# Two-layer transformer on one core: in the first attention, the visible parts of two key tiles share one 128-column row of scores, and GpSimd takes the weights apart again; weights are split two steps ahead

## The reference, cut to what matters

```
x = x + attn0(layernorm(x))          # x is (4, 512, 256) float32
q = einsum('btd,ndh->btnh', x, q_kernel)            # 16 heads of 128
k, v = einsum('bsd,ckdh->cbskh', x, kv_kernel)      # 8 key/value heads
q, k = rope(rms_norm(q)), rope(rms_norm(k))
mask = (j <= i) & (i - j < 128)                     # causal, window of 128
logits = where(mask, (q * scale) @ k, lowest)
out = softmax(logits) @ v @ out_kernel
```

## Time and profile before

| | |
|---|---|
| median of 3 runs | 1585.34 us (1585.33 to 1596.49) |
| the profiled execution | 1583.67 us, of which its span 1581.4 us |
| PE busy | 92% of the span |
| DVE / ACT / POOL busy | 70% / 51% / 21% of the span |
| first attention | from the start to about 653 us |
| mean granted TensorE clock | 0.958 of full speed |

### The profile page before, as it was taken

The page is one execution under the profiler, slowest core; times in us unless marked ns, Lnnn a source line. Parts: engine busy times, 40 slices in busy tenths (PEclk is TensorE's granted clock), DMA queues, the critical chain, the costliest instruction groups (busy, mean ns, idle before and its releaser), DMA issues.

```text
span 1581.4 us, 24555 instructions
## 1 busy us (share of the span) xinstructions
PE 1452.6 (92%) x7806; PEld 1104.6 (70%) x7806; DVE 1112.8 (70%) x2356; ACT 810.5 (51%) x1983; POOL 334.4 (21%) x448
## 2 busy tenths in 40 slices
PE   3699999999999999799999999999849898989898
PEld 2589989988998899667777777777624344444376
DVE  5699899989998999377555455455437676767554
ACT  2466676666766767444332332332215464646566
POOL 3364454444444544000000000000012020201000
PEclk9899999999999999899999999999957899999999
DMA  4210000000000000233000000000052232222001
GB/s 130 67 41 1 2 1 1 1 3 1 1 2 1 1 1 1 67 90 90 21 1 0 0 0 0 0 0 0 1 204 65 70 91 70 90 70 90 1 14 40
DMA packets 30796, 52.75 MB, mean 33 GB/s; under 512 B 4480, under 2 KB 12544, under 8 KB 30304
## 3 DMA queue, kind: packets, MB, share of 16 engines
q1 hardware_dynamic: 30288, 50.63, 10.3%
q0 software_dynamic: 400, 0.78, 0.3%
HBM read 37.49 MB, written 14.68 MB: 33 GB/s over the span
## 4 chain that ended last, share of the span: by engine, by line
PE 83%; DVE 7%; ACT 4%; issue 3%; DMA 2%; POOL 0%; SPq 0%; DVEq 0%; ACTq 0%; POOLq 0%
PE ps L1216 16%; PE ps L1218 15%; PE ps L1217 15%; PE ps L1254 6%; PE ps L1300 6%; PE ps L1491 4%; PE ps L1530 4%; PE ps L1331 3%; PE ps L1281 2%; PE ps L1618 2%; PE ps L1504 2%; PE ps L1367 1%; PE ps L1636 1%; PE ps L1292 1%; PE ps L1516 1%
## 5 line engine op out<-in xcount | busy, mean ns | idle before, releaser
L806 DVE TENSOR_REDUCE nm<-ps 128x1 f32<-128x512 f32 x256 | 167.6, 684 | 101.8 <-PE ps L1491 101.7
L1138 ACT ACTIVATE pT<-ps 128x512 f32<-128x512 f32 x256 | 145.9, 597 | 140.0 <-PE ps L1504 137.6
L1216 PE MATMUL ps<-xnT_lo,w1moe_hi 128*128 128x512 f32 x400 | 177.0, 443 | 4.7 <-DVE w2moe_lo L764 4.5
L399 POOL TENSOR_TENSOR ln_rs<-ln_ve,minus_half 128x4 f32<-128x4 f32 x12 | 13.6, 1131 | 775.2 <-DVE ln_ve L496 775.2
L1068 ACT ACTIVATE moe_act_hi<-sg 128x512 fp32r<-128x512 f32 x100 | 63.3, 633 | 191.0 <-DVE sg L741 191.0
L1217 PE MATMUL ps<-xnT_hi,w1moe_lo 128*128 128x512 f32 x400 | 160.5, 401 | 0.0
L1218 PE MATMUL ps<-xnT_hi,w1moe_hi 128*128 128x512 f32 x400 | 159.9, 400 | 0.0
L1216 PE MATMUL ps<-wqkv_lo,xnT_hi 128*128 128x512 f32 x256 | 128.1, 500 | 25.5 <-DVE wqkv_lo L549 25.5
L998 ACT ACTIVATE rope<-ps 128x384 f32<-128x384 f32 x128 | 62.9, 491 | 156.4 <-PE ps L1218 155.4
L731 DVE TENSOR_TENSOR sg<-ps,sg 128x512 f32<-128x512 f32 x100 | 69.0, 690 | 95.5 <-ACT sg L1088 95.3
L424 POOL TENSOR_TENSOR rope<-rope 128x384 f32<-128x384 f32 x128 | 131.7, 1029 | 0.0
(11 more groups left out here) (205 smaller groups left out, 3688.7 us busy)
## 6 DMA issues: line engine op xcount, KB each, us to landing
copies<-qk_hi SPq DMA_DIRECT2D x32, 256.0 KB
yT<-in_w1moe SPq DMA_DIRECT2D x25, 256.0 KB, 2.6
qst<-copies SPq DMA_DIRECT2D x64, 96.0 KB, 2.2
kst<-copies SPq DMA_DIRECT2D x64, 96.0 KB, 2.3
x_res<-in_wqkv SPq DMA_DIRECT2D x8, 512.0 KB, 3.7
copies<-qk_lo SPq DMA_DIRECT2D x16, 256.0 KB
w_in<-in_w2moe SPq DMA_DIRECT2D x25, 128.0 KB, 2.7
x_res<-in_wo SPq DMA_DIRECT2D x4, 512.0 KB, 3.8
```

Source lines behind the costliest of these rows:

```text
L806: V.tensor_reduce(nm1[:, n % 2, t, col:col + 1], ps[:, 1 + s1_slot(p), :], AX.X, ALU.max, negate=True).then_inc(s1_max, 1)
L1138: A(pT1[:, u % 2, 2 * (m % 2) + h, c, :], ps[:, 4 + e % 2, :], ACT.Exp, scale=SCALE1).then_inc(p1_ready, 1)
L1216: MM(out, left[0], right[1], start=first, stop=False)
```

## The change

1. Scores of the two key tiles go to two halves of each head's bank with no mask for two-tile groups (one-tile groups keep a mask, `causal`). DVE copies the older tile's half over the own tile's half where `older` (key > query) is set, in PSUM. Maxima, exponentials, row sums and scaling then run over 128 columns a head and not 256.
2. PE transposes 2 and not 4 blocks of weights. POOL writes two masked copies (`parted`) of the transposed weights with `affine_select`, one for each key tile, and PE multiplies these by the values. `attended` moves from lag 8 to lag 9, the output projection from 9 to 10.
3. ACT scales both heads; DVE's scaling of head 0 goes. DVE's subtraction for `enc_lo` moves ahead of the row maxima.
4. Chunks are split two steps ahead and ahead of the step's own work. POOL builds the rotary tables of tiles 1 to 3.

The diff, cut to its core:

```diff
-KV_RING, PROB_RING = 2 * GROUPS, 4
-LAST_LAG = 9
+K_RING, V_RING, PROB_RING, PART_RING = 2 * GROUPS, 4 * GROUPS, 4, 4
+LAST_LAG = 10
...
# SyncE
             load_chunk(0)
+            load_chunk(1)
...
+            sp.dma_start(older[:], dram["c_older"]).then_inc(older_loaded, 16)
...
# GpSimd
+            def part_probT(b, n, new, old):
+                m = n - 7
+                if (new if m >= 0 else old) and not alone(m):
+                    kb, s, r = b * STEPS + m, m % 2, m % PART_RING
+                    pool.wait_ge(probT_ready, kb + 1)
+                    if old or m >= PART_RING:
+                        pool.wait_ge(attended, kb - PART_RING + 1)
+                    if not isinstance(b, int):
+                        nc.gpsimd.tensor_tensor(idle[:], minus_half[:, 0:1], minus_half[:, 0:1], ALU.add)
+                    nc.gpsimd.affine_select(parted[:, r, 0], probT[:, s], [[0, 2], [-1, P]], ALU.is_gt, 0.0,
+                                            base=0, channel_multiplier=1)
+                    nc.gpsimd.affine_select(parted[:, r, 1], probT[:, s], [[0, 2], [1, P]], ALU.is_ge, 0.0,
+                                            base=0, channel_multiplier=-1).then_inc(probT_parted, 1)
             def attention_step(b, n, old, following):
+                part_probT(b, n, True, old)
...
             for n in range(STEPS):
                 attention_step(0, n, False, True)
-                if GROUPS <= n + 1 < CHUNKS:
-                    split_wo(n + 1)
+                if n + 1 < TT:
+                    tables(n + 1)
+                if GROUPS <= n + 2 < CHUNKS:
+                    split_wo(n + 2)
...
# VectorE
                 m = n - 6
...
                     V.reciprocal(rsums[:, s, :], psums[:, s, :]).then_inc(inv_ready, 1)
-                    dve.wait_ge(inv_ready, k + 1)
-                    V.tensor_tensor(prob[:, m % PROB_RING, 0, 0:w], prob[:, m % PROB_RING, 0, 0:w],
-                                    rsums[:, s, 0:1].to_broadcast((P, w)), ALU.mult).then_inc(normed[0], 1)
                 m = n - 4
...
-                    V.tensor_reduce(nmax[:, s, :], ps[:, 3 + s, :].rearrange("p (h f) -> p h f", h=2)[:, :, 0:w],
-                                    AX.X, ALU.max, negate=True).then_inc(max_ready, 1)
+                    if not alone(m):
+                        V.memset(spare[:, 1:2], 0.0)
+                        V.copy_predicated(bank[:, :, 1, :], older[:], bank[:, :, 0, :]).then_inc(merged, 1)
+                m = n - 9
...
+                    dve.wait_ge(enc_high, k + 1)
+                    V.tensor_tensor(enc[1][:, s, :], ps[:, 6, 0:2 * P], enc[0][:, s, :], ALU.subtract
+                                    ).then_inc(enc_split, 1)
+                m = n - 4
...
+                    V.tensor_reduce(nmax[:, s, :], bank[:, :, 1, :], AX.X, ALU.max, negate=True).then_inc(max_ready, 1)
...
             for n in range(STEPS):
+                if 2 <= n + 2 < GROUPS:
+                    split_wqkv(n + 2)
                 attention_step(0, n, True, False, True)
-                if n + 1 < GROUPS:
-                    split_wqkv(n + 1)
...
# ScalarE
-                    A(prob[:, m % PROB_RING, 1, 0:w], prob[:, m % PROB_RING, 1, 0:w], ACT.Copy, scale=rsums[:, s, 1:2]
-                      ).then_inc(normed[1], 1)
+                    for h in range(2):
+                        ins = A(prob[:, m % PROB_RING, h, :], prob[:, m % PROB_RING, h, :], ACT.Copy, scale=rsums[:, s, h:h + 1])
+                    ins.then_inc(normed, 1)
```

More of the change, by code:

```diff
@@ L101, in build @@
         ident_b = sb("ident_b", [P, P], BF16, part_a)
-        window = sb("window", [P, 2, 2, P], BF16, part_a)
+        idle = sb("idle", [P, 1], where=part_a)
+        causal = sb("causal", [P, 2, P], BF16, part_a)
+        older = sb("older", [P, 2, P], I32, part_a)
         qks = sb("qks", [P, 3, P], where=part_a)
@@ L322, in _ @@
             sp.dma_start(sin_in, dram["c_sin"]).then_inc(tables_loaded, 16)
-            for j in range(1, STAGES):
+            sp.dma_start(older[:], dram["c_older"]).then_inc(older_loaded, 16)
+            for j in range(2, STAGES):
                 load_chunk(j)
@@ L426, in attention_step, with tables @@
                     tile_rms(b, t + 1)
+            def tables(t):
+                h2 = HD0 // 2
+                three = lambda table, half: table[:, t:t + 1, half].to_broadcast((P, 3, half.stop - half.start))
+                nc.gpsimd.tensor_tensor(cos3[:, t], three(cos_in, slice(0, HD0)), qks[:], ALU.mult).then_inc(tables_ready, 1)
+                nc.gpsimd.tensor_tensor(sin3[:, t, :, 0:h2], three(sin_in, slice(0, h2)), qks[:, :, h2:HD0], ALU.mult
+                                        ).then_inc(tables_ready, 1)
+                nc.gpsimd.tensor_tensor(sin3[:, t, :, h2:HD0], three(sin_in, slice(h2, HD0)), qks[:, :, 0:h2], ALU.mult
+                                        ).then_inc(tables_ready, 1)
             tile_rms(0, 0)
+            pool.wait_ge(scales_ready, 2)
             for n in range(STEPS):
                 attention_step(0, n, False, True)
[L431 to L432 removed]
+                if n + 1 < TT:
+                    tables(n + 1)
+                if GROUPS <= n + 2 < CHUNKS:
+                    split_wo(n + 2)
             with pool.Fori(1, BATCHES - 1) as b:
@@ L439, in _ @@
                     rstd(0)
+            for n in range(LAST_LAG):
+                part_probT(BATCHES, n, False, True)
             pool.wait_ge(out0_added, BATCHES * TT)
@@ L619, in attention_step @@
                     dve.wait_ge(v0_kept, k + 1)
+                    if not old and g == 0 and t > 0:
+                        dve.wait_ge(tables_ready, 3 * t)
                     V.tensor_tensor(rope1[:, s, :], ps[:, s, 0:3 * P], cos3[:, t, :, :].rearrange("p h f -> p (h f)"), ALU.mult)
@@ L1019, in attention_step @@
                 if valid(m):
-                    k, s, w = k0 + m, m % 2, seen(m)
+                    k, s = k0 + m, m % 2
                     act.wait_ge(max_ready, k + 1)
+                    if not old and m == 0:
+                        act.wait_ge(tables_ready, 3 * (TT - 1))
                     if old or m >= 2:
@@ L1321, in attention_step @@
                 if valid(m):
-                    k, both = k0 + m, seen(m) > P
-                    for h in range(2):
-                        pe.wait_ge(normed[h], k + 1)
+                    k = k0 + m
+                    pe.wait_ge(normed, k + 1)
                     if old or m >= 1:
```

153 lines of the change are left out of this document (83 added, 70 removed).

## The result

The changed kernel takes 1534.41 us (median of 4 runs, 1532.77 to 1536.40); the kernel before, on the same chip, 1587.10 (4 runs, 1585.33 to 1596.49). The ratio is 0.9651, 95% interval 0.9614 to 0.9689. The profiled execution took 1534.22 us with a span of 1532.4, at a mean granted clock of 0.957. So the change brings 49.0 us of span, where 44 were forecast.

A forecast was written before the change was run, and what follows sets the result against it. PE was taken to bound full steps, with DVE close behind; 24 us from three loop sequences plus 23 from sequence 0 less 3 reserve made 44 us off 1585.3, so 1541 us, range 1524 to 1592.

The forecast's parts named there:

- PE sets the pace, 4.40 a full step: Full attention steps: PE, busy without a gap, loses mask product and two transposes, 4.84 to 4.40 us.
- A sequence of the loop at 138.9: Sequences 1 to 3: PE's steps sum to 136.5 us plus 2.4 of waits for ACT, against 146.90.
- the 24: Sequences 1, 2 and 3 of the loop: a gain of 8.0 us each, 24 us together.
- ACT's second scaling, 0.3 of waiting in n = 3 to 10: Steps with short scores: PE waits 0.3 us for ACT's second scaling before its transposes, 2.4 us a sequence.
- The select at 0.70: POOL's two selects a step: 0.70 us each, low end 0.41, making POOL's step 4.0 us, under PE's 4.40.
- the choice between the bounds: PE or POOL pacing steps: POOL's 2.60 + 2X exceeds 4.40 above X = 0.90; POOL rival 1602 us, chance 0.18.
- the reserve of 3 us for POOL: Taken off the total gain for POOL's one-column powers beside selects and DVE's waits on a running select.
- DVE's swap at nothing: DVE's scaling of head 0 goes, a predicated copy (0.41 us) and memset come: no cost on the path.
- What it gives back lies in the short steps, where DVE was the one without idle time: Short steps: relief from DVE's swap falls there, said to be already in the sum, which goes by PE alone.
- The early steps, 18 us: Start of sequence 0: weights split ahead; steps 0 to 5 take 31.5 us, 18 of sequence 0's 23 us gain.
- Step 0 begins where it does: Start of the kernel: no gain, as the first projection still hangs on chunk 0 and the masks.
- The drain at nothing, plus or minus 2: End of the attention: one more step but each shorter, taken as nothing, plus or minus 2 us.

The follow-up runs named there:

- the best version: The kernel after with ACT's two scalings ahead of its squares and the product with the values at lag 8, not 9: 1520.31 us, ratio 0.9568.
- the two scaling experiments: The kernel before with both heads scaled on ACT and DVE's scaling gone: 1596.07 us; the same with the scalings ahead of ACT's squares: 1583.02 us.
- e4: The kernel after with the product with the values at lag 8 in place of 9: 1532.67 us, ratio 0.9643.
- e9: The kernel after with its chunks of weights split one step late again, at the end of a step: 1551.21 us, ratio 0.9757.
- e7: The kernel after with four more selects a step on POOL, six in all: 1546.99 us, ratio 0.9733.
- e1: The kernel before with only the scaling moved: ACT scales both heads, DVE's scaling goes: 1596.07 us, ratio 1.0047.
- e10: The kernel before with both scalings on ACT, placed ahead of ACT's squares: 1583.02 us, ratio 0.9955.
- e6: The kernel after with two more selects a step on POOL, four in all: 1535.82 us, ratio 0.9653.
- e8: The kernel after with the mask product and the transposes given back to PE: 1575.87 us, ratio 0.9885.
- e2: The kernel before with chunks of weights split two steps ahead and chunk 1 loaded first: 1574.16 us, ratio 0.9882.
- e5: The kernel after with ACT's scalings ahead of its squares and lag 8 for the product with the values: 1520.31 us, ratio 0.9568.
- e3: The kernel after with ACT's two scalings ahead of its squares of the new projection: 1525.25 us, ratio 0.9587.

## Why the prediction was right, and where its terms were off

- **PE sets the pace, 4.40 a full step**: measured 4.40, and 4.83 with the removed work given back. Right.
- **A sequence of the loop at 138.9**: sequence 2 took 139.12 in place of 146.90. Two of its terms were off and partly cancel: the transposes of a new input tile add 0.42 each time and not 0.22, since PE now reaches them before ACT has copied q and k (at n = 21 of sequence 2 the copy ends at 392.45 and they start at 392.58; with the mask product given back they add 0.22 again, 5.05 against 4.83), and the steps with a short product take 3.97 and not 4.06. Sequence 1 took 144.71, since the passage of the loop falls into it; the sum priced the passage as unchanged and it grew by 2.5 (5.6 against 3.1), mostly by the low clock behind it. The three sequences gave 21.7 of the 24.
- **ACT's second scaling, 0.3 of waiting in n = 3 to 10**: 0.28 at 320.89, and 3.97 in the short steps in place of 3.70. Right, for seven of the eight steps, and it is most of what the best version takes back.
- **The select at 0.70**: it is 0.41, with a spacing of 0.36. This term was mis-sized in the choice between the bounds: I let a computed index and comparison weigh against half of L424's two-input rate, and that low end (0.41) is what was measured; one agreement makes no rule of it. L465's 1.225, the only one-input row, is no measure of a select. The Trainium skill (GPSIMD Engine Reference, Engine selection) calls one-input work roughly line rate; the 0.2 us estimated from that is nearer than my 0.70, but half of what was measured. The time did not hang on the price up to 0.72, as four selects a step showed, and no wait of PE in the loop takes up the reserve of 3 us for POOL.
- **DVE's swap at nothing**: right in the full steps. The predicated copy is 0.425, and DVE then idles 1.10 before `enc_lo` in the step at 291.05.
- **"What it gives back lies in the short steps, where DVE was the one without idle time"**: wrong, as the two scaling experiments show: 0.6 to 1.0 us a sequence. The sum goes by PE alone and does not hold it.
- **The early steps, 18 us**: steps 0 to 5 took 27.5 us where 31.5 were forecast, so the term was mis-sized by 4.0 us: in steps 0 to 2 POOL runs back to back (5.32, 5.43 and 5.14 us a step, for its own work and the tables) and the sums of DVE stand 14.55 us apart over three steps, where 18 were taken; steps 3 to 5 took 12.96 in place of 13.5. The four steps with POOL's chunks took 21.65 (21.35 forecast), and the rest 93.1 (95.1). Together sequence 0 is 142.2 and not 147.9. The 18 itself compares unlike things: it is 49.66 us of seven steps (0 to 6) less 31.5 for six. Like for like, steps 0 to 5 fell from 42.3 to 27.5, 14.8 us where 10.8 were forecast. The sum of the sequence is not touched by this, since its other two terms have the shifted steps.
- **Step 0 begins where it does**: it began 2.1 us earlier, and the term was put at nothing because the first projection hangs on the masks. It does, but the mask lands earlier. PE's first wait was for `window`, 9.8 us, and is now for `causal`, 7.6 us. With the splits ahead and chunk 1 loaded first it is 8.4 in the kernel with `window`; with the splits late in the kernel with `causal` it is 9.2. So most of it goes with the part that loads and splits ahead and less with the smaller mask; why, no run separates.
- **The drain at nothing, plus or minus 2**: 2.1 longer, at the edge.

The terms that were off, by the profiled executions, are sequence 0 +5.7, the start +2.1 and the unused reserve +3, against the loop -2.3, the drain -2.1 and -1.2 after the attention. That makes +5.2, and the span's gain exceeds 44 by 5.0 (the rest is rounding). So the mechanism was right, and that the sum came within 5 us is in part luck: 10.8 us of misses one way stood against 5.6 the other way.

## What to carry to other kernels

Where one engine fills its step without a gap, sum that engine's instructions and check that each of the others stays below it; here work taken off an engine that was only nearly as busy brought next to nothing, and put in the wrong place elsewhere it costs. A result that the busiest engine needs late in its step belongs at the front of its producer's program, not behind work that waits for this step. When an unseen instruction must be priced, rows of other instructions give bounds and not a price (here 0.41 and 1.225 for what took 0.41), so ask up to which price the forecast stands. And compare steps on the engine that is full: the periods of another one (3.96 against 3.70 before, 4.72 against mostly 4.40 with six selects) can be longer for a while and be made up later.

## What was not expected of the hardware

- `affine_select` on GpSimd over 256 float32 columns takes 0.41 us (0.36 from start to start), while L465, one input and two per-partition scalars over as many columns, takes 1.225.
- Behind the passage of the loop PE ran at the lower clock in six of the twelve traces of this study and at the full clock in the other six. The waits of PE there were 3.60 (after), 3.55 (e4), 3.37 (e9), 3.28 (e7), 3.01 (e1) and 1.98 us (e10) in the first six, and 3.50 (e6), 3.01 (e8), 2.90 (e2), 2.86 (before), 2.08 (e5) and 1.72 us (e3) in the others. So the wait's length does not decide it: 3.01 us stands on both sides. With each kernel traced once, what does stays open, and also whether it is the same in every execution. The price is read from the two steps around the passage: beyond the wait they lose 1.9 to 3.0 us at the lower clock, 0.3 to 0.5 at the full one. The first 3.5 us behind the two waits of 3.01 us, e1 and then e8 (granted clock third from the end):

```profile
335.29:338.80 3.51, 3.51 (x8) 2.81 (x9) 0.42 (x1) 0.38 (x1) 0.00 (x0) 0.50 0.02 5
```

```profile
314.06:317.56 3.50, 3.50 (x20) 3.05 (x21) 1.98 (x7) 1.53 (x5) 0.91 (x3) 1.00 0.02 7
```

- A GpSimd instruction that overlaps one of DVE with two inputs in SBUF takes up to twice its time: a select 0.76 in place of 0.40 (at 245.79 with six selects a step), L449 1.72 in place of 0.86 and L451 1.87 in place of 1.00 in the first steps. It goes the other way too: DVE's L659 took 2.73 in place of 0.55 at 56.36, where POOL's L422, started at 56.29, took 2.39.
